# A transformer block on one core: the convolution's taps move to ScalarE, all score products to VectorE

## The reference, cut to what matters

```
x = x + LN(xn + attn(xn)),  xn = LN(x)
x = x + LN(ffn(LN(x)))

attn: q, k, v = split(xn @ Wqkv); 8 heads of 16
  scores of token s: q_s . k_{s-off}/4 for off in 0, 1, 2, 4, ... 512 (negative positions masked)
  tele = softmax over the 11 offsets, times v_{s-off}
  conv = causal depthwise convolution of v with 7 taps per channel
  low  = linear attention with features elu + 1
  attn = (tele + conv + low) @ Wo
ffn: 8 experts of hidden size 64, the 2 best per token by sigmoid gates, and a shared expert; exact gelu
```

## Time and profile before

| | us |
|---|---|
| median of 3 runs | 341.38 |
| span of the profiled execution | 339.5 |
| TensorE matmul busy | 261.4 |
| VectorE busy | 275.6 |
| ScalarE busy | 176.8 |
| GpSimd busy | 196.6 |

### The profile page before, as it was taken

One profiled execution on the slowest core, in us unless ns is written; L12 is line 12 of the kernel. 1 busy time (PEld: TensorE's weight loads), 2 busy tenths in 40 slices (PEclk: granted clock), 3 DMA queues, 4 the chain that ended last, 5 costly groups with the idle time before them and its releaser, 6 DMA issues.

```text
span 339.5 us, 4554 instructions
## 1 busy us (share of the span) xinstructions
PE 261.4 (77%) x1527; PEld 175.7 (52%) x1527; DVE 275.6 (81%) x555; ACT 176.8 (52%) x443; POOL 196.6 (58%) x193
## 2 busy tenths in 40 slices
PE   6666667089379699997788499998795878888894
PEld 6323342087334537667455237767443277685374
DVE  5079866188999999989999999989999999845752
ACT  1683055302538755593569344775484606176852
POOL 4960999601889995306899980327979943131013
PEclk9785996569879959999999659999999559989999
DMA  7200376000025700200049300100248200000003
GB/s 219 71 0 16 106 196 147 24 0 3 9 90 143 215 26 8 69 26 3 37 130 229 111 12 2 31 2 8 84 124 215 83 12 31 0 2 0 2 2 93
DMA packets 20038, 21.89 MB, mean 64 GB/s; under 512 B 3289, under 2 KB 16434, under 8 KB 20014
## 3 DMA queue, kind: packets, MB, share of 16 engines
q1 hardware_dynamic: 20014, 21.59, 22.9%
HBM read 5.07 MB, written 2.10 MB: 21 GB/s over the span
## 4 chain that ended last, share of the span: by engine, by line
DVE 48%; PE 24%; ACT 9%; SPq 7%; DMA 6%; issue 4%; POOL 2%; POOLq 0%; DVEq 0%; ACTq 0%
DVE prods L263 12%; PE psH L1195 7%; DVE prods L880 6%; SPq L340 5%; DMA v_shift<-v_tok 5%; PE psA L1113 3%; DVE hid L994 3%; PE psY L1206 2%; PE psY L1292 2%; PE psA L1105 2%; DVE wgt L853 2%; PE psG L1278 2%; DVE gtmp L966 2%; SPq L339 2%; DVE gtmp L979 2%
## 5 line engine op out<-in xcount | busy, mean ns | idle before, releaser
L421 POOL TENSOR_SCALAR var<-ss 128x4 f32<-128x4 f32 (+1 forms) x25 | 13.4, 538 | 98.9 <-ACT squares L603 46.6
L263 DVE TENSOR_TENSOR prods<-qT,kT 128x1024 f32<-128x1024 f32 x32 | 55.4, 1778 | 12.4 <-ACT qT L530 12.4
L460 POOL TENSOR_TENSOR convT<-convT,tapT 128x1024 f32<-128x1024 f32 x24 | 57.9, 2412 | 2.0
L1195 PE MATMUL psH<-ident,prods 128*128 128x128 f32 x324 | 44.6, 290 | 0.0
L263 POOL TENSOR_TENSOR prods<-qT,kT 128x1024 f32<-128x1024 f32 (+1 forms) x12 | 28.8, 2418 | 23.2 <-PE psA L1163 11.3
L1195 PEld LDWEIGHTS psH<-ident,prods 128*128 128x128 f32 x324 | 40.5, 152 | 2.3 <-issue 2.3
L423 POOL TENSOR_TENSOR rstd<-var,neg_half 128x4 f32<-128x4 f32 (+2 forms) x29 | 37.8, 1305 | 2.4
L1163 PE MATMUL psA<-prods,slot_sel 128*32 128x512 f32 x168 | 26.0, 676 | 12.9 <-DVE prods L263 12.6
L880 DVE TENSOR_TENSOR prods<-v_shift,wgt 128x896 f32<-128x896 f32 x32 | 34.7, 1083 | 0.0
L880 DVE TENSOR_TENSOR prods<-v_tok,wgt 128x128 f32<-128x128 f32 (+2 forms) x60 | 25.8, 456 | 9.9 <-DMA v_shift<-v_tok 9.9
L1113 PE MATMUL psA<-xnT,wqkv 128*128 128x512 f32 x48 | 29.9, 767 | 5.0 <-ACT xnT L530 5.0
(11 more groups left out here) (194 smaller groups left out, 581.3 us busy)
## 6 DMA issues: line engine op xcount, KB each, us to landing
x_in<-L_attn_x SPq DMA_DIRECT2D x4, 512.0 KB, 4.0
x_res<-L_attn_x SPq DMA_DIRECT2D x4, 512.0 KB, 15.3
v_shift<-v_tok SPq DMA_DIRECT2D x4, 508.0 KB
v_shift<-v_tok SPq DMA_DIRECT2D x4, 504.0 KB
v_shift<-v_tok SPq DMA_DIRECT2D x4, 496.0 KB
v_shift<-v_tok SPq DMA_DIRECT2D x4, 480.0 KB
v_shift<-v_tok SPq DMA_DIRECT2D x4, 448.0 KB
out<-y_out SPq DMA_DIRECT2D x7, 256.0 KB, 2.3
```

Of the source, the lines that this page charges most:

```text
L263: return eng.tensor_tensor(prods[:, QUADS * (s % 2) + q, t0:T], qT[:, t0:T], kT[:, PRE - off + t0:PRE - off + T], ALU.mult)
L460: conv_chain(nc.gpsimd.tensor_tensor(convT[:], convT[:], tapT[:], ALU.add))
L1195: ins = pe.matmul(dst, terms[:, j % TERM_BUFS, m, :], ident[:], is_transpose=True, start=False, stop=(m == live[-1]))
```

## The change

ScalarE scales vT by all seven taps (`scale_taps`). It has no seven free tiles, so `TAP_HOME` gives each tap a home among tiles that are idle then: convT, tapT, qexp, xnT, kexp, and tapT and kexp once more for taps 5 and 6, which must wait until GpSimd has added taps 1 and 4. Five taps are scaled after keep_normed, two after normalise1(b+1). GpSimd only adds (`sum_taps`), where the convolution stood. VectorE does all eleven products, and one more gate step stands beside them. evacuate_x and features get waits on tap_added.

```diff
-POOL_PRODUCTS = ((1, 0), (1, 1), (2, 0))
+TAP_HOME = (0, 1, 2, 3, 4, 1, 4)
+N_ADDS = TAPS - 1
-N_PRODUCTS = (4, 6, 8)
+N_PRODUCTS = (4, 8, 11)
+        def tap_buf(i):
+            return (convT, tapT, qexp, xnT, kexp)[i][:]
 @block.gpsimd
-            def products(b, slots):
...
-            def conv_start(b):
...
-            def conv_taps(b, shifts):
...
+            def sum_taps(b, taps):
+                for tap in taps:
+                    pool.wait_ge(tap_scaled, upto(b, TAPS, tap + 1))
+                    pool.wait_ge(tap_added, upto(b, N_ADDS, tap - 1))
+                    nc.gpsimd.tensor_tensor(convT[:], convT[:], tap_buf(TAP_HOME[tap]), ALU.add).then_inc(tap_added, 1)
...
-            products(0, (1,))
             for b in range(B + 1):
-                if attn:
-                    products(b, (2,))
                 if more:
                     ln1(b + 1)
                 if ffn and attn:
                     ln3(u1)
                 if attn:
-                    conv_start(b)
-                    conv_taps(b, range(1, TAPS))
-                    conv_chain.done()
+                    sum_taps(b, range(1, TAPS))
...
-                if more:
-                    products(b + 1, (1,))
 @block.scalar
             def evacuate_x(b):
+                if b:
+                    act.wait_ge(tap_added, upto(b - 1, N_ADDS, 3))
             def evacuate_v(b):
-                act.wait_ge(conv_step, upto(b, N_CONV_STEPS, 0))
+            def scale_taps(b, shifts):
+                for shift in shifts:
+                    if shift == 0 and b == 0:
+                        act.wait_ge(conv_ld, 16)
+                    if shift == 0:
+                        act.wait_ge(hT_ready, upto(b, 2, 0))
+                    elif shift == 2:
+                        act.wait_ge(fq_ready, upto(b, 1, 1))
+                    elif shift == 4:
+                        act.wait_ge(fk_ready, upto(b, 1, 1))
+                    elif shift == 5:
+                        act.wait_ge(tap_added, upto(b, N_ADDS, 1))
+                    elif shift == 6:
+                        act.wait_ge(tap_added, upto(b, N_ADDS, 4))
+                    nc.scalar.activation(tap_buf(TAP_HOME[shift]), vT[:, VPRE - shift:VPRE - shift + T], ACT.Copy,
+                                         scale=cw[:, TAPS - 1 - shift:TAPS - shift]).then_inc(tap_scaled, 1)
             def features(b):
+                act.wait_ge(tap_added, upto(b, N_ADDS, 0))
...
                     keep_normed(b)
+                    scale_taps(b, range(0, 5))
                     if ffn:
                         norm3_squares(u1)
...
                     if more:
                         normalise1(b + 1, range(TPH if b else 0, NT))
+                    scale_taps(b, range(5, TAPS))
                     if ffn:
                         normalise3(u1)
 @block.vector
-                mine = [q for q in range(QUADS) if TERMS[SLOTS * q + s] != LOW and (s, q) not in POOL_PRODUCTS]
+                mine = [q for q in range(QUADS) if TERMS[SLOTS * q + s] != LOW]
...
-                dve.wait_ge(conv_step, upto(b, N_CONV_STEPS, N_CONV_STEPS))
+                dve.wait_ge(tap_added, upto(b, N_ADDS, N_ADDS))
...
-                    linear_state(b, gate_step_of(u0, 2 if more else 0))
+                    linear_state(b, gate_step_of(u0, 3 if more else 0))
-                        gates(u0, range(4 if more else 2, 24))
+                        gates(u0, range(5 if more else 2, 24))
 @block.tensor
             def sum_heads(b, s):
-                if s:
-                    pe.wait_ge(pool_prod_ready, upto(b, len(POOL_PRODUCTS), s + 1))
```

More of the change, by code:

```diff
@@ L61 @@
 PSA_AHEAD = 2 * 4
-N_PRODUCTS = (4, 6, 8)
+N_PRODUCTS = (4, 8, 11)
 N_SOFTMAX_STEPS = 5
-N_CONV_STEPS = 2 * TAPS - 1
 N_FRONT = 3
@@ L240, in block_kernel @@
         v_shifted, low_ready, low_used = sem("v_shifted"), sem("low_ready"), sem("low_used")
-        pool_prod_ready = sem("pool_prod_ready")
         terms_ready, terms_summed = sem("terms_ready"), sem("terms_summed")
-        conv_step, hT_ready, y_ready, yc_ready = sem("conv_step"), sem("hT_ready"), sem("y_ready"), sem("yc_ready")
+        tap_scaled, tap_added = sem("tap_scaled"), sem("tap_added")
+        hT_ready, y_ready, yc_ready = sem("hT_ready"), sem("y_ready"), sem("yc_ready")
         ss2_ready, x2_ready, ss3_ready, xn3_ready = sem("ss2_ready"), sem("x2_ready"), sem("ss3_ready"), sem("xn3_ready")
@@ L253, in block_kernel @@
         softmax_chain = Chain(softmax_step, N_SOFTMAX_STEPS)
-        conv_chain = Chain(conv_step, N_CONV_STEPS)
         def bank(tile):
             return tile // TPH, bass.ts(tile % TPH, P)
+        def tap_buf(i):
+            return (convT, tapT, qexp, xnT, kexp)[i][:]
         def product(eng, s, q):
```

## The result

The changed kernel takes 356.68 us (median; 351.95 to 358.40) against 341.36 us for the kernel before on the same chip: ratio 1.037, 95% interval 1.029 to 1.045. It is 3.7% slower. The profiled execution took 355.27 us, its span is 353.5 us, 14.0 more than before. (In two of the four executions the granted clock was lower, 0.85 and 0.86 against 0.88 and 0.90; the ratio leaves them out, the median does not.)

What follows compares the result with a forecast made beforehand. No single bound: VectorE led, the end handed between engines; ScalarE's slack before gT decided. Span 339.5 + 11.1 (15.8 - 1.0 - 2.5 - 1.2) + 1.9 around it = 352.5, said as 352 us; range 345 to 358.

Steps and rivals of the forecast that it cites:

- Products and gate steps: VectorE, batches 1 to 3: all products there, net -2.1 us a batch; gate steps end earlier, no longer meeting the convolution.
- Taps at 0.95 us: ScalarE: seven tap activations of 128x1024 at 0.95 us each, 6.65 us a batch, bounds 0.9 and 1.1.
- First consequence: ScalarE, batch 1: gate_logits ends some 2.1 us earlier, but five taps put norm3_squares and everything behind it 2.5 us late.
- Second consequence: GpSimd's adds start late, behind ln3, 2.45 us apart; ScalarE stands 3.6 us at tap 6 in batch 1.
- gT: ScalarE's turned gates come 5.8, 2.2 and 7.8 us later in batches 1 to 3, sum +15.8 us.
- What comes back: Savings against the delay: TensorE's transposes 1.0 us, VectorE's softmax weights 2.5, first weighings 1.2.
- Batch 0: Logits 7 us later, but VectorE is still ready before the shift DMA; taken as 0, up to 1.6 us gain possible.
- Rival A: Fourth add is over when ScalarE reaches tap 6, so it does not stand there; 338 us, chance 0.08.
- Rival B: VectorE last at the logits: the products' 2.1 us come off batches 1 to 3, 335 us, chance 0.04.
- Rival C: Adds waiting for VectorE's products and logits delay tap 6 by 2.3 us a batch; about 359 us, chance 0.13.

Runs made afterwards that it cites:

- own home: Changed kernel with tap 6 written to idle scratch squares4 instead of kexp, so its wait for the fourth add is gone: 336.65 us, ratio 0.989.
- last taps late: Changed kernel with taps 5 and 6 moved on ScalarE from ahead of normalise3(u1) to behind the softmax's exponentials: 336.48 us, ratio 0.991.
- the first experiment: The same run as own home: changed kernel with tap 6 in squares4 instead of kexp, 336.65 us, ratio 0.989.
- without the hold: Changed kernel with own tiles for taps 5 and 6, taps 0 to 3 in ScalarE's gaps, GpSimd's adds not held back: 340.44 us, ratio 1.003.
- Gaps and hold together: Same as without the hold, but GpSimd's adds are kept back until VectorE's 24 gate steps are done: 329.95 us, ratio 0.971.
- squares first: Changed kernel with norm3_squares(u1) ahead of the five taps on ScalarE, tap 6 still in kexp: 342.13 us, ratio 1.004.
- half adds: Changed kernel with GpSimd adding only the first 512 of 1024 columns, half of the convolution's sum left out: 339.92 us, ratio 1.000.

## Why the prediction was right, and which of its terms were off

The forecast was 352 us; the profiled execution took 355.27, the median is 356.68, both inside the range of 345 to 358 near its upper end. The mechanism is the one forecast, ScalarE standing at tap 6 with normalise3 and gT behind it, and three experiments show it from three sides: without the wait (own home), with the wait moved behind what it held up (last taps late), and with the adds that it waits for cut in half. Each lands at 336 to 340 us. The number is nearer than its terms: 5.9 us too few were put ahead of gT, and 3.0 us too few were given back, so that two misses partly cancel.

*Products and gate steps* (net -2.1 us on VectorE, gate steps without the 2.2 us ones): right for batch 1. Four products take 4.62 us, all of a batch 12.29 instead of 14.32, and no gate step was stretched. In batch 2 the products fit (12.27 instead of 14.34), but the claim that the gate steps no longer meet the adds is wrong: the first add starts at 187.11 and three casts (187.24, 189.76, 192.26) take 2.23 to 2.26 us each, so the gates end at 194.5, 30.4 us into the batch instead of the 22.9 forecast. It cost nothing only because normalise3 stood later still, at 198.04. In batch 3 the products gave nothing back, 12.12 us instead of 12.04: before, only the first two GpSimd products met them there.

*Taps at 0.95 us*: too low. They stand 1.04 us apart, within the bounds given (0.9 to 1.1), 0.6 us more a batch. The nearest row was an activation with a constant scale; these read the scale from a tile. The Trainium skill has it (ScalarE: Activation LUTs, What ACT_TABLE_LOAD costs): a pointer operand of one value a partition adds about 93 ns. The rows agree, 1.14 us for a tap against 1.04 for Relu.

*First consequence* (gate_logits 2.1 us earlier in batch 1): wrong. The products did end earlier, but keep_normed started 15.6 us into the batch, as it had before (15.7). TensorE used the time up. Its rows in the changed kernel:

```profile
90.56 3.64 PE L1159 MATMUL psA<-prods,slot_sel 128*32 128x512 f32 x16 [2.98 <-DVE prods L267]
...
96.32 2.07 PE L1231 MATMUL psF<-x3T,w 128*128 128x512 f32 x2 [0.69 <-ACT x3T L506]
98.19 2.78 PE L1140 MATMUL psY<-v_tok,fk_tok 128*128 128x128 f32 x16
```

Before, the last two took 1.12 and 1.95 us, and the four matmuls of turn_x3 ahead of them 0.66 us against 1.11 after. The granted clock of two stretches there (us, busy time and count of PE, PEld, DVE, ACT, POOL; PEclk; DMA share; GB/s), first after, then before:

```profile
94.50:98.20 3.70, 2.99 (x7) 1.56 (x8) 3.70 (x5) 0.60 (x1) 3.55 (x3) 0.50 0.26 85
```

```profile
98.00:100.20 2.20, 1.51 (x6) 0.83 (x7) 2.20 (x2) 0.60 (x1) 2.08 (x1) 1.00 0.68 214
```

0.50 is the level of 1.2 GHz, 1.00 that of 2.4. In both kernels the clock was low behind the idle time ahead of sum_heads; before, it was back when gate_logits' matmuls came, after, it was not. This cost the 2.0 us that the step had taken off.

*Second consequence* (adds from ln3 on at 2.45 us, ScalarE stands at tap 6): right, and the largest term. Measured: pitch 2.49, first add to end of the fourth 9.84 us (forecast 9.80), ScalarE idle 3.83 us in batch 1 (forecast 3.6).

*gT*, +5.8, +2.2 and +7.8 us: measured from the start of each batch +8.9, +3.2 and +9.6. Batch 1's missing 3.1 are the 2.0 above, 0.4 for five taps, 0.4 in TensorE's turn between normalise3 and gT, and 0.2 of the adds and tap 6. Batch 3's 1.8 are 0.4 for a later keep_normed, 0.3 for the taps, 0.6 for an add of 2.87 us that met VectorE's logits, and 0.5 as in batch 1. Batch 2's 1.0 I haven't split. So the term of 15.8 us measured 21.7.

*What comes back*: 4.7 us forecast, 6.6 measured; wgt took 0.96 us in all three batches, below the 1.16 that I took, which is 0.6 of the difference; the other 1.3 us are not placed. *Batch 0*, forecast at 0 with up to 1.6 below, gave 1.1; its first weighing waited 4.2 us for the DMA, so the cover held.

339.5 + 21.7 - 6.6 - 1.1 = 353.5, the span. The remaining 1.4 us between the profiled execution and the median are the spread of executions.

*Rival A* (ScalarE does not stand, 338) was wrong for this kernel. The kernel with a home of its own is that case, at 336.65, but the near agreement is luck: rival A had 1.4 us more ahead of gT and 4.7 given back behind it. Against the kernel before, the profiled execution has 6.4 us more ahead of gT (3.7, -1.1 and 3.8), 9.4 less behind it and 1.6 less before batch 1. *Rival B* (VectorE's relief reaches the end) was wrong for this kernel too, but real in the products alone: with the taps left on GpSimd 4 us came off (I had 6, a third of it in batch 3, where the products gave nothing back). The condition given for it, a short wait for tap 6, is what the first experiment made true. *Rival C* (adds that wait for VectorE) delayed tap 6 in one place only, by the 2.87 us add of batch 3; in batches 1 and 2 the add that waited, 2.88 us, came behind the fourth.

Undoing the wait gave back 18.6 us of span, more than its 14.5 us of idle time, and 5 us more than was expected of that experiment. gT comes 15.3 us earlier over the three batches (39.8 + 37.9 + 39.0 against 34.7 + 33.5 + 33.2). And TensorE's busy time fell from 265.3 to 256.2 us for the same 1527 matmuls: more of them ran at the higher level of the clock (mean 0.883 and 0.912). How much of that is caused by the wait and how much is the difference between two executions stays open; two executions of the changed kernel differ by 3.3 us at mean clocks of 0.883 and 0.896.

## What to carry to other kernels

ScalarE took its jobs in the order of its program: at tap 6 it stood 3.83 to 6.86 us with normalise3 ready behind it. So a wait for a buffer that is used again costs whatever stands behind it: before giving a reused tile to an engine, list the jobs queued behind its wait, and look for scratch that is idle just then, or put the write where the readers are long done. Work moved to the least busy engine fits best into the gaps that its timeline shows, but here the gaps alone gave nothing: without the hold that kernel is at ratio 1.003, behind the 0.989 of the block with a home of its own. Gaps and hold together gave 0.971; the block with a hold was not run. And once GpSimd has a free choice of when to run large two-input work, hold it until VectorE's short two-input steps are over: here one such hold was worth 10.5 us.

## What the runs showed of the hardware

**Short VectorE instructions lose whole GpSimd instructions.** A two-input gate step on 128x32 takes 0.19 us alone and 2.06 to 2.37 when it starts just behind an add. RECIPROCAL at 111.92, inside an add, took its usual 0.18 us, and the reduction of the logits took 1.54 to 1.56 us beside an add or not. The step on 128x4 at 111.72 took 0.16 us, but it began 0.06 us ahead of the next add; begun 0.16 us behind one (batch 3 with the squares first, the add from 255.47) it is stretched like the others:

```profile
255.63 2.19 DVE L967 TENSOR_TENSOR gmax<-gmax 128x4 f32<-128x4 f32 x1
```

What I had not expected is that a cast from f32 to bf16, with one input, waited as well (2.33 us here, and the three of 2.23 to 2.26 us in batch 2 of the changed kernel). The Trainium skill states both (SBUF — State Buffer, Who interferes with whom): reductions never contend, and a cast may, in a mode that takes both ports. The rows agree. And the loser of a pair is whichever came second: an add took 2.87 us instead of 2.35 behind a VectorE instruction of the logits.

**The clock eats small gains.** A saving ahead of a TensorE that has been idle was undone by the lower clock. The same 16 matmuls took 3.64 us in batch 1 of the changed kernel and 1.92 us with tap 6 in its own home, behind the same 2.98 us of idle time:

```profile
90.08 1.92 PE L1158 MATMUL psA<-prods,slot_sel 128*32 128x512 f32 x16 [2.98 <-DVE prods L267]
```

The granted clock of these two stretches (PEclk, the number ahead of the DMA share), changed kernel first:

```profile
90.50:94.20 3.70, 3.64 (x16) 0.59 (x16) 3.67 (x19) 1.83 (x8) 3.37 (x6) 0.50 0.06 27
```

```profile
90.05:92.05 2.00, 1.92 (x16) 0.42 (x16) 2.00 (x6) 0.43 (x4) 1.89 (x2) 1.00 0.06 27
```

With the same 2.98 us of idle time the 16 matmuls took 2.47 us with the squares first, 2.51 with the last taps late, 1.92 with half adds, 3.29 and 1.92 in the gaps with and without the hold. So the idle time alone doesn't tell the level, and the rows don't show what does. In the changed kernel and the four experiments that have its order of jobs up to there (own home, squares first, last taps late, half adds), keep_normed starts 14.8 to 16.5 us into batch 1, so a difference of up to 1.7 us in a single column of batch 1 is not by itself the work of an edit. A forecast of a stage with matmuls behind an idle time needs both prices.
